# A graph layer in tiles of 128 nodes, with the adjacency built from pairs of nodes and one chunk of 128 edge slots

## The reference

```python
xn = layernorm(x)
# graph convolution, twice: D = diag(1/sqrt(degree)), A = adjacency with counts, with one more loop per node
z  = relu(D A D (xn @ W1) + b1)
z  = relu(D A D (z @ W2) + b2)
q, k, v = split(xn @ W_qkv + b_qkv)            # centred and squared, then normed to q2, k2
mix = (v + q2 @ (k2.T @ v) / sqrt(N)) @ W_out + b_out
x1 = x + z + mix
w  = softmax over 64 slices of 8 heads of layernorm(x1) @ W_logits
out = x1 + w @ M                                # M: from w.T @ layernorm(x1), by a small attention over the slices
```

## Time and profile before

| | |
|---|---|
| median of three runs | 2424.62 us |
| span of the profiled execution | 2418.1 us (what lies around the span is not in the profile; the median is 6.5 us above it) |
| busy share of the span | PE 88%, PEld 52%, DVE 67%, ACT 50%, POOL 11% |
| setup | 0 to 120.5 us |
| layernorm and q, k | 120.5 to 328 us |
| stream 0 | 345 to 490 us |
| graph layer 1 | 493 to 1450 us |
| graph layer 2 | 1451 to 2240 us |
| stream 1, after the small attention | 2278 us to the end |

### The profile page before, as it was taken

The page is one execution under the profiler, slowest core; times in us unless marked ns, Lnnn a source line. Parts: engine busy times, 40 slices in busy tenths (PEclk is TensorE's granted clock), DMA queues, the critical chain, the costliest instruction groups (busy, mean ns, idle before and its releaser), DMA issues. The chain is left out here.

```text
span 2418.1 us, 46873 instructions
## 1 busy us (share of the span) xinstructions
PE 2138.7 (88%) x11593; PEld 1261.3 (52%) x11593; DVE 1617.6 (67%) x6548; ACT 1204.1 (50%) x2836; POOL 265.0 (11%) x362
## 2 busy tenths in 40 slices
PE   4199967769999999999999998999999999998676
PEld 3156645535555555555555554555555555554554
DVE  4877741189999999999999963555555555555211
ACT  0156630058888888888888861333333333333000
POOL 4300002220000000000000001000000000000122
PEclk7599989979999999999999999999999999999799
DMA  2123325512112111221122115444444444442255
GB/s 70 26 85 97 96 86 182 184 58 93 83 82 110 82 83 82 106 86 82 83 103 89 82 82 186 142 142 141 140 140 140 139 138 141 139 141 79 75 185 168
DMA packets 106114, 268.90 MB, mean 111 GB/s; under 512 B 14324, under 2 KB 91422, under 8 KB 93164
## 3 DMA queue, kind: packets, MB, share of 16 engines
q1 hardware_dynamic: 75456, 230.75, 27.2%
q10 hardware_dynamic: 26700, 32.01, 3.8%
q0 software_dynamic: 3808, 4.76, 0.7%
HBM read 140.70 MB, written 126.75 MB: 111 GB/s over the span
## 5 line engine op out<-in xcount | busy, mean ns | idle before, releaser
L1222 DVE TENSOR_SCALAR big<-big,key_hi 128x250 f16<-128x250 f16 x2500 | 695.6, 295 | 48.7 <-PE ps L1269 44.2
L1280 PE MATMUL ps<-hs,at 128*128 128x512 f16 x2500 | 722.9, 378 | 0.6 <-POOL at L1193 0.6
L1500 PE MATMUL ps<-big,at 128*128 128x512 f16 x2500 | 581.9, 380 | 6.5 <-DMA at<-at_scratch 6.5
L1225 DVE TENSOR_SCALAR big<-big,key_lo 128x128 f16<-128x128 f16 x2000 | 529.0, 264 | 0.0
L1269 PE MATMUL ps<-big 128*128 128x250 f16 x2500 | 472.3, 275 | 53.1 <-DVE big L1225 42.4
L1330 ACT CAST at<-ps 128x500 f16<-128x500 f32 (+1 forms) x650 | 427.9, 683 | 137.5 <-PE ps L1269 137.3
L1269 PEld LDWEIGHTS ps<-big 128*128 128x128 f16 x2500 | 223.4, 97 | 363.6 <-ACT at L1330 71.8
L1500 PEld LDWEIGHTS ps<-big,at 128*128 128x128 f16 x2500 | 242.4, 98 | 265.9 <-issue 10.8
L1280 PEld LDWEIGHTS ps<-hs,at 128*128 128x128 f16 x2500 | 240.5, 97 | 59.7 <-POOL at L1193 6.5
L1344 ACT ACTIVATE big<-big,key_lo 128x128 f16<-128x128 f16 x500 | 172.3, 395 | 169.4 <-POOL big L1177 155.7
L1348 ACT ACTIVATE big<-big,ones 128x128 f16<-128x128 f16 x500 | 173.4, 394 | 8.1
(11 more groups left out here) (265 smaller groups left out, 2399.7 us busy)
## 6 DMA issues: line engine op xcount, KB each, us to landing
at_scratch<-at SPq DMA_DIRECT2D x50, 1600.0 KB, 5.4
at<-at_scratch SPq DMA_DIRECT2D x50, 1600.0 KB, 7.2
big<-in_x_dram SPq DMA_DIRECT2D x100, 125.0 KB
xT_scratch<-big SPq DMA_DIRECT2D x100, 125.0 KB, 1.9
big<-xT_scratch SPq DMA_DIRECT2D x50, 250.0 KB
wT_scratch<-big ACTq DMA_DIRECT2D x50, 250.0 KB, 2.5
hs<-wT_scratch SPq DMA_DIRECT2D x50, 250.0 KB
base_scratch<-big ACTq DMA_DIRECT2D x50, 125.0 KB
```

What stands on the lines that cost most here:

```text
L1222: last = v.tensor_scalar(hot_hi[:, s, c, :], iota_hi, key_hi[:, bass.ds(w, 1), c], None, ALU.is_equal)
L1225: last = v.tensor_scalar(hot_lo[:, s, c, :], iota_lo, key_lo[:, bass.ds(w, 1), c], None, ALU.is_equal)
L1280: mm = te.matmul(ps[:, 2 + b, :], lhsT=at[:, b, k * P:(k + 1) * P], rhs=hs[:, k, :], start=(k == 0), stop=(k == T - 1))
L1500: mm = te.matmul(ps[:, b, :], lhsT=at[:, b, k * P:(k + 1) * P], rhs=hs2[:, k, :], start=(k == 0), stop=(k == T - 1))
```

## The change

A tile is now 128 nodes, so T = 49 with a last tile of 106 nodes (`rows(t)`). A window is a pair of nodes (WIN = 2) with 128 slots (CAP), one chunk; there are 64 windows a tile (WPT) and NW = 3136. Both keys are 16-bit now.

**One-hots.** Eight pairs are handled by one comparison (BW = 8). The one-hot of a batch is laid out with the pair innermost: element (k, w) at 8k + w. DVE runs a TENSOR_TENSOR with both inputs in 16 bits, the row of numbers repeated eightfold and the keys read again for every k. There are two of them a batch (784 and 1024 elements), eight batches a tile, and a ring of four batches. ACT makes none.

**Build.** A pair is one matmul of 98 columns. Its two operands are read from the batch's one-hots with a step of eight elements, 16 bytes. Four pairs share a bank (UW = 4), 16 units are a tile, and the banks 0, 1, 6, 7 take turns. `aggregate` has 49 matmuls a tile, dealt over the pairs from i = 4 on.

**Setup.** Eight nodes (SUPER) are looked up together, with 384 targets each (SCAP), in seven groups of 112 (G, GW). Nine sums of comparisons for each group give the number of edges below each node: five on DVE, four on ACT. From them come the degrees and the first edge of every pair, and POOL then fetches the 128 sources of each pair with 28 indirect DMAs, from a padded copy of the source list (`src_dram`). The keys are made in passes over 3584 elements per partition. The large clearings on POOL, of `hs` in setup and of `big_f` in layer 1, are gone or shrunk to one tile.

```diff
-    rounds = (tiles - 1) // unroll
+    rounds = (tiles - 1 - lead) // unroll
...
-    NT = 125
-    T = N // NT
-    WIN = 5
+    NT = P
+    T = -(-N // NT)
+    LAST = N - (T - 1) * NT
+    NODES = T * NT
+    WIN = 2
+    CAP = P
+    SUPER = 8
+    WPS = SUPER // WIN
+    SCAP = 384
+    GW = 112
+    G = NODES // SUPER // GW
     WPT = NT // WIN
     NW = T * WPT
-    CHUNKS = 2
-    CAP = CHUNKS * P
-    GW = 125
-    G = NW // GW
     KC = T * WIN
+    BW = 8
+    BATCHES_T = WPT // BW
+    UW = 4
+    UNITS = WPT // UW
...
-                for to, of, s in ((dstg, dst, dst_gathered), (srcg, src, src_gathered)):
-                    for g in range(G):
-                        pool.indirect_dma_start(
-                            out=to[:, g, :], out_offset=None, in_=of.rearrange("(e a) -> e a", a=1),
-                            in_offset=bass.IndirectOffsetOnAxis(ap=lo[:, g:g + 1], axis=0)).then_inc(s, 16)
-                pool.wait_ge(src_gathered, 16 * G)
+                for g in range(G):
+                    pool.indirect_dma_start(
+                        out=dstg[:, g, :], out_offset=None, in_=dst.rearrange("(e a) -> e a", a=1),
+                        in_offset=bass.IndirectOffsetOnAxis(ap=lo[:, g:g + 1], axis=0)).then_inc(dst_gathered, 16)
                 pool.wait_ge(dst_gathered, 16 * G)
+                pool.wait_ge(cut_ready, 1)
+                pool.wait_ge(src_padded, 32)
+                for n in range(G * WPS):
+                    pool.indirect_dma_start(
+                        out=srcg[:, n, :], out_offset=None, in_=src_dram.rearrange("(e a) -> e a", a=1),
+                        in_offset=bass.IndirectOffsetOnAxis(ap=wlo[:, n // WPS, n % WPS:n % WPS + 1], axis=0)
+                    ).then_inc(src_gathered, 16)
+                pool.wait_ge(src_gathered, 16 * G * WPS)
...
-                nc.gpsimd.memset(hs_f32[96:P, :], 0.0)
+                nc.gpsimd.memset(hs_f32[96:P, (T - 1) * C:T * C], 0.0)
...
+                for g in range(G):
+                    act.wait_ge(dl_ready, g + 1)
+                    for j in range(CUTS_V, SUPER + 1):
+                        n = g * (SUPER + 1 - CUTS_V) + j - CUTS_V
+                        if n >= 2:
+                            act.wait_ge(act_counted, n - 1)
+                        a.activation(junk_a[:, n % 2, :], dl[:, g, :], ACT.Sign, bias=below[:, j:j + 1],
+                                     accum_out=sums[:, g, j:j + 1]).then_inc(act_counted, 1)
...
-                g.memset(big_f[96:P, 0:T * C], 0.0).then_inc(pads_ready, 1)
-                pool.wait_ge(pads_ready, 3)
...
-                    w, s = t * WPT + i, i % RING
-                    if reached(w, RING):
-                        dve.wait_ge(built, w - RING + 1)
-                    for c in range(CHUNKS):
-                        last = v.tensor_scalar(hot_hi[:, s, c, :], iota_hi, key_hi[:, bass.ds(w, 1), c], None,
-                                               ALU.is_equal)
-                        if i not in ACT_LO:
-                            last = v.tensor_scalar(hot_lo[:, s, c, :], iota_lo, key_lo[:, bass.ds(w, 1), c], None,
-                                                   ALU.is_equal)
+                    n, s = t * BATCHES_T + i, i % RING
+                    if reached(n, RING):
+                        dve.wait_ge(built, (n - RING + 1) * BW)
+                    for keys, iota, hot, width in ((key_hi, iota_hi, hot_hi, KC), (key_lo, iota_lo, hot_lo, P)):
+                        last = v.tensor_tensor(hot[:, s, :].rearrange("p (k w) -> p k w", w=BW), iota,
+                                               keys[:, bass.ds(n * BW, BW)].rearrange("p (o w) -> p o w", o=1)
+                                               .to_broadcast([P, width, BW]), ALU.is_equal)
                     last.then_inc(hot_ready, 1)
...
-                    for c in range(CHUNKS):
-                        mm = te.matmul(ps[:, (b * UNITS + i // 2) % 2, i % 2 * KC:(i % 2 + 1) * KC],
-                                       lhsT=hot_lo[:, s, c, :], rhs=hot_hi[:, s, c, :],
-                                       start=(c == 0), stop=(c == CHUNKS - 1))
-                    mm.then_inc(built, 1)
+                    n, s, unit = t * BATCHES_T + i // BW, i // BW % RING, t * UNITS + i // UW
+                    if i % BW == 0:
+                        pe.wait_ge(hot_ready, n + 1)
+                    if i % UW == 0 and reached(unit, len(BANKS)):
+                        pe.wait_ge(at_stored, unit - len(BANKS) + 1)
+                    te.matmul(ps[:, BANKS[i // UW % len(BANKS)], i % UW * KC:(i % UW + 1) * KC],
+                              lhsT=hot_lo[:, s, :].rearrange("p (k w) -> p k w", w=BW)[:, :, i % BW],
+                              rhs=hot_hi[:, s, :].rearrange("p (k w) -> p k w", w=BW)[:, :, i % BW],
+                              start=True, stop=True).then_inc(built, 1)
...
-                        if reached(t, 0) and within(t, T) and i >= 2:
-                            aggregate(t, b, range((i - 2) * T // (WPT - 2), (i - 1) * T // (WPT - 2)))
+                        if reached(t, 0) and within(t, T) and i >= 4:
+                            aggregate(t, b, range((i - 4) * T // (WPT - 4), (i - 3) * T // (WPT - 4)))
...
-                    here = min(2, WPT - 2 * m)
-                    act.wait_ge(built, t * WPT + 2 * m + here)
+                    act.wait_ge(built, t * WPT + (m + 1) * UW)
...
-                def low_hots(t, n):
```

More of the change, by code:

```diff
@@ L309, in _ @@
                 dve.wait_ge(iotas_ready, 1)
+                step(v.tensor_scalar(below, below, -1.0, 0.5, ALU.mult, ALU.add))
                 for c in range(HC):
@@ L366, in _ @@
                 for g in range(G):
[L367 to L371, removed]
-                        v.tensor_scalar(junk[:, n % 4, :], dl[:, g, :], float(j), 0.0, ALU.is_equal, ALU.add,
-                                        accum_out=deg[:, g, j:j + 1]).then_inc(deg_counted, 1)
@@ new lines, in _, with over @@
+                v.tensor_copy(wlo, wlo_f).then_inc(cut_ready, 1)
+                dve.wait_ge(deg_made, 1)
+                pairs = deg.rearrange("p g (w j) -> p g w j", j=WIN)
+                step(v.tensor_tensor(many, pairs[:, :, :, 0], pairs[:, :, :, 1], ALU.add))
+                step(v.tensor_scalar(some, many, float(CAP), None, ALU.min))
+                v.tensor_reduce(small[0:GW, 0:1], some.rearrange("p g w -> p (g w)"), AX.X, ALU.add).then_inc(deg_ready, 1)
+                def over(y):
+                    return y.rearrange("p (w o) -> p w o", o=1).to_broadcast([GW, G * WPS, CAP])
@@ new lines, in _ @@
+                slots = slot.rearrange("p (o s) -> p o s", o=1).to_broadcast([GW, G * WPS, CAP])
+                step(v.tensor_tensor(held, slots, over(many.rearrange("p g w -> p (g w)")), ALU.is_lt))
+                step(v.tensor_copy(some, pairs[:, :, :, 0]))
+                dve.wait_ge(src_gathered, 16 * G * WPS)
+                step(v.tensor_scalar(src_lo, srcg, P - 1, None, ALU.bitwise_and))
+                v.scalar_tensor_tensor(out=keyl, in0=src_lo, scalar=1.0, in1=held, op0=ALU.add, op1=ALU.mult
@@ L383, in _ @@
                                        ).then_inc(keys_made, 1)
+                step(v.tensor_scalar(tile_of, srcg, 7, None, ALU.logical_shift_right))
                 dve.wait_ge(keys_made, 1)
-                dve.wait_ge(deg_counted, G * WIN)
-                v.scalar_tensor_tensor(out=dl, in0=tile_of, scalar=float(WIN), in1=dl, op0=ALU.mult, op1=ALU.add
+                step(v.tensor_tensor(held, slots, over(some.rearrange("p g w -> p (g w)")), ALU.is_ge))
+                v.scalar_tensor_tensor(out=keyh, in0=tile_of, scalar=float(WIN), in1=held, op0=ALU.mult, op1=ALU.add
@@ L449, in _ @@
                 pe.wait_ge(deg_ready, 1)
-                t.matmul(ps[0:1, 0, 0:1], lhsT=small[:, 0:1], rhs=ones[:, 0:1], start=True, stop=True).then_inc(deg_turned, 1)
+                t.matmul(ps[0:1, 0, 0:1], lhsT=small[0:GW, 0:1], rhs=ones[0:GW, 0:1], start=True, stop=True).then_inc(deg_turned, 1)
             @block.scalar
@@ L762, in std @@
                     act.wait_ge(ln_step, 2 * t + 2)
-                    a.activation(rstd[0:NT, b:b + 1], mv[0:NT, b, 1:2], ACT.Sqrt, bias=eps[0:NT, 0:1]).then_inc(std_ready, 1)
+                    a.activation(rstd[0:rows(t), b:b + 1], mv[0:rows(t), b, 1:2], ACT.Sqrt, bias=eps[0:rows(t), 0:1]).then_inc(std_ready, 1)
                 def keep(t, b, u):
@@ L1409, in gps_layer @@
         w_acc = take([P, HB, NT])
[L1410 removed]
+        take = carve(key_hi[:, :].bitcast(F32))
         w2 = take([P, CB, C])
```

301 lines of the change are left out of this document (151 added, 150 removed).

## The result

| | us, median | runs | ratio to before, 95% |
|---|---|---|---|
| before | 2424.8 | 2423.4 to 2426.7 | |
| changed | 2530.0 | 2527.9 to 2530.7 | 1.0426 [1.0412, 1.0441] |

What follows compares the result with a forecast made beforehand. PE was taken to bound both layers, with DVE also near its limit in layer 1. Terms -38 - 16 - 24 - 6 + 24 = -60 us took the 2418.1 us span to 2358, median 2364; eight-in-ten range 2245 to 2430.

Steps and rivals of the forecast that it cites:

- the price of a build: Layer 1, PE: a build with stepped operands costs 0.084 us, or 0.110 behind another build, 5.8 us a tile.
- The upper end: Layer 1 builds: one store-like jump of 1.3 ns per column would make a build 0.17 us.
- rival C: Build's moving operand: a step costs TensorE ACT's jump in ns; builds 0.17 us, tile 23.3, total 2626; chance 0.14.
- Aggregates at 0.216 us: Layer 1, PE: 49 aggregates at 0.216 us each from start to start, 10.57 us a tile.
- The seam under C: Between two layer 1 tiles, with builds at 0.17 us: almost no waiting, 0.1 us, against the forecast's own 0.6.
- DVE at half the 32-bit rate: Layer 1 comparisons in 16 bits: 0.47 and 0.60 us a batch, 9.3 us a tile, hidden behind PE.
- ACT hidden: Layer 1, ACT: 16 stores of 392 elements a tile, at most 12.6 us, hidden.
- Rival A: Layer 1 builds: steps are free, a build costs 0.055 us, a tile 15.95, total 2264 us; chance 0.27.
- Start of layer 1: Layer 1's first tile: POOL's clearing goes, and 29.3 us become 13.5, giving -16 us.
- Layer 2: Layer 2, all PE: one tile and one aggregate a tile fewer, slightly wider tiles, giving -24 us.
- Setup: Setup with new sums, fetches and key passes: +24 us; +10 with fetches closer together, +35 if weights hold DVE.
- The streams: The two streams, a tile fewer each, move the same bytes and so gain only -2 us together.

Runs made afterwards that it cites:

- e1: Changed kernel, only each build matmul reads both operands as one contiguous slice, so only times are of use: 2159.2 us, ratio to before 0.8914.
- e3: Changed kernel, only the builds' weights read contiguously, the moving operand still stepping 16 bytes; only times are of use: 2523.2 us, ratio to before 1.0420.
- sweep: Changed kernel with contiguous build weights and the moving operand read in turn with steps of 1, 2, 4, 8, 16 and 32 elements: 2390.8 us, one execution.
- e9: Changed kernel with GpSimd's clearing of 12544 elements put back after the number rows of layer 1: 2529.6 us, one execution.
- e8: Changed kernel with one-hots contiguous pair by pair, keys doubled, and later aggregates, earlier copy and later turn: 2085.4 us, ratio to before 0.8610.
- e6: Kernel before, only that both streams load the residual in 128 rows in place of 125: 2352.0 us, ratio to before 0.9709.

## Why the prediction was wrong

**The failed step** is the price of a build, "I take one extra column time per column, 2 x 0.041 + 0.002 = 0.084 us". It costs 0.155 to 0.159 us, 1.14 ns a column above the contiguous 0.043 (e1, e3, sweep), and the aggregate behind it 0.021 more, which no term had. The upper end was near: the store's jump of 1.1 to 1.3 ns gave 0.17 us. I scaled it by element times to 0.10 us (the 0.83 ns an element that I used isn't in those rows, which have 500 elements in 575 ns) and then went below that, towards the end without any penalty, with no row for it. The price turned out close to the nearest row in ns. That a write by ScalarE and a read by TensorE cost nearly the same per jump is luck as far as these runs go; nothing in them ties the two together.

**What followed** is rival C: 0.17 us a build, 23.3 us a tile; measured 0.159 and 23.22. The mechanism is C's, but so close a sum is partly luck: 64 builds take 10.3 us where C had 11.6, the aggregates 11.6 where it had 10.57, and a wait of 0.4 us ahead of the multiplication stood in no sum. C had a chance of 0.14 and lay outside the range. Its total of 2626 was 96 us too high, and that is nearly the streams.

**Layer 1, the rest.** Aggregates at 0.216 us: right wherever the build ahead is contiguous. The seam under C, 0.1 us: right, PE waits 0.6 us in all for the loops. DVE at half the 32-bit rate: right, 0.48 and 0.60 us from start to start where 0.47 and 0.60 stood; the two elements a cycle that the Trainium skill (VectorE: DVE Perf Modes, The perf-mode tier table) gives agree. ACT hidden: right. Rival A's tile of 15.95 us with free steps is e1's 15.68.

**Start of layer 1.** From DVE's first comparison to the first aggregate it is 13.9 us; the forecast's 13.5 had 1.1 us of number rows in it, so 12.4. The number rows for eight pairs take 1.51 and 1.93 us on GpSimd where 0.37 and 0.24 stood before, 2.8 us more in place of 1.1, and they begin 4.9 us behind the stream's last add where it was 3.6. So the stage gained 11.8 and not 16. The trace of before shows the clearing holding DVE, as I wrote, but its going wasn't what the changed kernel needed (e9).

**Layer 2**, -24 forecast, -11.5 measured. The aggregate that went was cover:

```profile
1905.30 0.75 DVE L1629 SCALAR_TENSOR_TENSOR big<-ps,small,blogb 128x512 f32<-128x512 f32 x1 [3.43 <-PE ps L1551]
1910.61 0.41 DVE L1597 TENSOR_TENSOR big<-ps,big 128x256 f32<-128x256 f32 x1
1911.07 0.44 PE L1527 MATMUL ps<-ident,big 128*128 128x128 f32 x2 [0.17 <-DVE big L1597]
```

From the last aggregate's start to this turn it is 0.56 us where it was 0.24 before: some 0.31 us a tile, 15 us. The chain runs through VectorE: PE's logits (L1551), the softmax from L1629 on, `gather` (L1597) behind it, the turn. Between logits and turn PE has 18 aggregates where it had 19, 0.216 us less of cover, and from L1629 to `gather` it is 5.32 us where it was 5.21; together that is the 0.31. e8 has 19 aggregates there again, by putting the turn two later and the logits one later. It gets 7 us back: its turn still waits the 0.1 us that the softmax grew by, and in some tiles the x turn now waits.

**Setup**, +24 forecast, +10 measured; +10 was named for fetches closer together, and they are: 1.24 us from one to the next of 112 rows, where 1.51 was read for 125 rows.

```profile
35.42 0.93 POOL L308 DMA_INDIRECT big<-in_dst_dram,big  x1 [0.30 <-issue]
36.66 0.93 POOL L308 DMA_INDIRECT big<-in_dst_dram,big  x1 [0.30 <-issue]
```

35 of them make 9.5 us, and the first came at 31.35 and not at 35. The traces tell that it is the number of rows and not their length: before, 125 rows took 1.51 us with 125 elements a row (L273) and with 256 (L280); now 112 rows take 1.24 us with 125 elements (L302), 384 (L308) and 128 (L315).

**The streams**, -2 forecast, -90 measured: "which move the same bytes" looked at bytes where the number of engines that a transfer reaches was the bound (e6, which alone takes 71 us off the kernel before). The trace of before showed it: waits for loads at a DMA share of 0.59. This miss hid part of the other: layer 1 came out 256 us above its forecast, the whole only 166.

## What to carry to other kernels

Lay what TensorE streams as its moving operand out contiguously: a step of 16 bytes made 98 columns cost 155 ns in place of 43, while the same step in the weights hid. Let the vector comparison work in the order that gives this layout; with each key doubled it lost nothing. Where DMA is waited for at a share well under 1, look at whether the outer dimension divides among the engines, and keep the price of the nearest row inside the range that you give for an unmeasured access. That its price in ns came so close is this one case's result.

## What the runs showed of the hardware that I had not expected

- The moving operand's price by step: 0.43, 0.47, 0.70, 1.58, 1.60 and 1.52 ns a column for steps of 2, 4, 8, 16, 32 and 64 bytes; a weight load with a step of 16 bytes 145 ns against 99.
- A matmul behind one whose moving operand had a step of 8 bytes or more starts its follower 21 ns later (0.237 against 0.216 us).
- GpSimd's MEMSET of 10.76 us held a 16-bit TENSOR_SCALAR for its whole length, and one of 10.61 us a 16-bit TENSOR_TENSOR not at all (e9). The Trainium skill (SBUF — State Buffer, Who interferes with whom) says this of the two kinds of instruction; the runs agree.
- Transfers of 125 rows of 1024 bytes had never over 7 packets in flight; widening one of two such transfers to 128 rows took a stream's tile from 2.72 to 2.04 us.
- GpSimd's indirect fetches came every 1.51 us with 125 rows and every 1.24 us with 112, for rows of 125 to 384 elements.
